# Cross-attention and a ternary feed-forward on one core: one f16 cast from VectorE to ScalarE, row maxima in PSUM, new instruction orders, feed-forward two steps earlier

## The reference

```
h = layernorm(x)
q = rmsnorm(h @ Wq) * gq ;  k = rmsnorm(ctx @ Wk) * gk ;  v = ctx @ Wv        # by head, D = 128
P = softmax(q @ k.T / sqrt(D))
x = x + (P @ v) @ Wo
y = quant8(layernorm(x)) ;  g = y @ tern(w_gate).T ;  u = y @ tern(w_up).T
h = rms_norm(silu(g) * u) * ln_weight
x = x + quant8(h) @ tern(w_down).T
```

## Time and profile before

| | |
|---|---|
| median of the runs | 529.06 us |
| profiled execution | 530.74 us, span 528.9 us |
| mean granted TensorE clock | 0.974 |
| PE busy | 420.7 us (80%) |
| weight loads busy | 316.9 us (60%) |
| DVE busy | 484.6 us (92%) |
| ACT busy | 428.1 us (81%) |
| POOL busy | 386.8 us (73%) |

### The profile page before, as it was taken

The page is one execution under the profiler, slowest core; times in us unless marked ns, Lnnn a source line. Parts: engine busy times, 40 slices in busy tenths (PEclk is TensorE's granted clock), DMA queues, the critical chain, the costliest instruction groups (busy, mean ns, idle before and its releaser), DMA issues.

```text
span 528.9 us, 14416 instructions
## 1 busy us (share of the span) xinstructions
PE 420.7 (80%) x4456; PEld 316.9 (60%) x4456; DVE 484.6 (92%) x1303; ACT 428.1 (81%) x1447; POOL 386.8 (73%) x312
## 2 busy tenths in 40 slices
PE   0248275699999999999999999999999556678885
PEld 0137264577777777677776777777777343345554
DVE  1989969899999999999999999999999857899995
ACT  1079488498988989889898898988989638799983
POOL 1015628479989899998989999899989943666772
PEclk9999877799999999999999999999999999899999
DMA  7950713154734445354444535445464530000001
GB/s 278 347 170 22 233 46 81 41 81 85 155 79 100 99 91 108 79 114 85 99 99 84 114 79 111 87 95 104 89 114 85 117 60 2 1 20 32 30 30 51
DMA packets 145324, 50.16 MB, mean 95 GB/s; under 512 B 135952, under 2 KB 143120, under 8 KB 144784
## 3 DMA queue, kind: packets, MB, share of 16 engines
q1 hardware_dynamic: 144192, 46.68, 39.7%
q10 hardware_dynamic: 1104, 3.15, 1.7%
HBM read 14.16 MB, written 2.10 MB: 31 GB/s over the span
## 4 chain that ended last, share of the span: by engine, by line
DVE 48%; issue 29%; POOL 11%; PE 5%; DMA 3%; ACT 3%; DVEq 1%; POOLq 0%; ACTq 0%
DVE khl L855 9%; DVE khl L837 5%; DVE qhl L812 3%; POOL work L476 3%; DVE smax L808 3%; POOL qshl L482 3%; POOL rkq L497 3%; DVE ham L914 2%; DVE nbias L820 2%; DVE ohl L830 2%; DVE work L979 2%; DMA xs<-in_x 2%; DVE phl L843 2%; DVE kqe L848 1%; PE KQ L1128 1%
## 5 line engine op out<-in xcount | busy, mean ns | idle before, releaser
L576 ACT ACTIVATE work<-SO,nbias,rkq 128x128 f32<-128x128 f32 x256 | 115.1, 479 | 23.9 <-DVE nbias L820 23.8
L351 PE MATMUL KQ<-hT,wqs 128*128 (+1 forms) x1536 | 104.3, 226 | 19.3 <-DVE qhl L812 7.2
L497 POOL TENSOR_TENSOR rkq<-kqe,negh 128x8 f32<-128x8 f32 x65 | 108.6, 1670 | 13.6 <-DVE kqe L848 13.6
L351 PEld LDWEIGHTS KQ<-hT,wqs 128*128 128x128 f16 x1536 | 95.0, 101 | 28.5 <-DVE qhl L812 11.0
L488 POOL TENSOR_TENSOR phl<-work,phl 128x512 f16<-128x512 f32 x64 | 74.1, 1158 | 45.3 <-DVE phl L843 45.3
L351 PE MATMUL EB<-As,ohl 128*128 128x256 f16 x768 | 94.3, 273 | 0.0
L351 PEld LDWEIGHTS EB<-As,ohl 128*128 128x128 f16 x768 | 75.0, 98 | 21.5 <-issue 0.2
L476 POOL TENSOR_TENSOR work<-work,rinv 128x512 f32<-128x512 f32 x64 | 70.0, 1094 | 7.2 <-DVE rinv L789 7.2
L482 POOL TENSOR_TENSOR qshl<-work,qshl 128x512 f16<-128x512 f32 x64 | 75.2, 1174 | 0.1
L351 PE MATMUL SO<-pT,cs 128*128 128x512 f16 x192 | 53.0, 386 | 11.5 <-DMA pT<-phl 10.5
L351 PE MATMUL SO<-kT,qhl 128*128 128x128 f16 x768 | 54.7, 222 | 9.0 <-ACT work L576 6.6
(11 more groups left out here) (159 smaller groups left out, 945.0 us busy)
## 6 DMA issues: line engine op xcount, KB each, us to landing
xs<-in_x SPq DMA_DIRECT2D x4, 512.0 KB, 10.6
wvo<-in_wo SPq DMA_DIRECT2D x1, 2048.0 KB, 18.9
out<-wqs SPq DMA_DIRECT2D x16, 128.0 KB, 1.7
raw<-in_ctxT ACTq DMA_DIRECT2D x1, 1024.0 KB, 5.5
stage<-in_wk SPq DMA_DIRECT2D x1, 1024.0 KB, 13.4
stage<-in_wq SPq DMA_DIRECT2D x1, 1024.0 KB, 16.3
stage<-in_wq ACTq DMA_DIRECT2D x1, 1024.0 KB, 12.7
kT<-khl SPq DMA_TRANSPOSE x64, 2.9
```

The lines of the kernel that those rows point to most:

```text
L351: last = matmul(out, lhsT=left(i), rhs=right(j), start=start and n == 0, stop=stop and n == 2)
L497: pool.tensor_tensor(rkq[:, g % 4, :], kqe[:, g % 2, :], negh[:, 0:2 * HG], ALU.pow).then_inc(root_ok, 1)
L576: ins = act.activation(pe[:, s, c], SB[:, c], ACT.Exp, scale=rkq[:, (g - AT_X + 1) % 4, HG + h:HG + h + 1], bias=nbias[:, s, h:h + 1], acc ...
```

## The change

P's high half is made by ACT (L625 of the changed kernel, the last instruction of its turn) and no longer by DVE. From turn 8 on `smax` lies in PSUM (`smax_ps`), and two constants lie there too (`c_psum`, set by DVE in turn 7), with which `pss` and `kqe` of k are formed; before, they were immediate numbers. All engines' blocks stand in another order inside a turn. The feed-forward begins with turn 66 instead of 68 and runs six of its turns beside the attention's last; for it GU writes `KQ` and `TM`, the hidden transposes `SO`, and the second part of the layer norm's statistics is two turns later.

```diff
-FFN_AT = NT + AT_O - AT_GU
+FFN_AT = NT + AT_X - AT_GU
...
-        smax = sb("smax", [P, 2, HG])
+        smax_sb = sb("smax", [P, 2, HG])
...
+        c_psum = TPf[:, 16:16 + 2 * HG].rearrange("p (s h) -> p s h", s=2)
+        smax_ps = TPf[:, 0:2 * HG].rearrange("p (s h) -> p s h", s=2)
+
+        def smax_of(b, s):
+            return smax_sb[:, s, :] if isinstance(b, int) and b < 2 else smax_ps[:, s, :]
...
-            for s in range(G):
-                step((FFN_AT + s) // G, (FFN_AT + s) % G)
-                ffn(0, s)
-            straight(ffn, G, 2 * G)
+            for s in range(2 * G):
+                if FFN_AT + s < NT + AT_E + 1:
+                    step((FFN_AT + s) // G, (FFN_AT + s) % G)
+                ffn(s // G, s % G)
...
+                if live(b, g, 0):
+                    s = g % 2
+                    need(pool, qsq_ok, b, g, 0)
+                    need(pool, ssq_ps, b, g, 0, 2)
+                    pool.tensor_tensor(qshl[:, s, 1, :], qsq[:, s, :], qshl[:, s, 0, :],
+                                       ALU.subtract).then_inc(qslo_ok, 1)
...
-                if live(b, g, 0):
-                    s = g % 2
-                    need(pool, qsq_ok, b, g, 0)
-                    need(pool, ssq_ps, b, g, 0, 2)
-                    pool.tensor_tensor(qshl[:, s, 1, :], qsq[:, s, :], qshl[:, s, 0, :],
-                                       ALU.subtract).then_inc(qslo_ok, 1)
...
-                if now(b, g) == G:
+                if now(b, g) == G + 2:
                     ffn_roots(1)
...
+                split(now(b, g))
...
+                if live(b, g, AT_X):
+                    s = (g - AT_X) % 2
+                    need(act, pn_ok, b, g, AT_X)
+                    need_dma(act, pT_in[s], b, g, AT_X, 2)
+                    act.copy(phl[:, s, 0, :], pn[:, s, :]).then_inc(phi_ok, 1)
...
+                    if now(b, g) == AT_GU:
+                        act.wait_ge(plo_ok, NT)
...
                     need(dve, pn_ok, b, g, AT_X, 2)
-                    dve.tensor_scalar(pss[:, s, :], psm[:, s, :], 1.0 / P_SCALE, None, ALU.mult).then_inc(pss_ok, 1)
+                    if isinstance(b, int) and b < 2:
+                        dve.tensor_scalar(pss[:, s, :], psm[:, s, :], 1.0 / P_SCALE, None,
+                                          ALU.mult).then_inc(pss_ok, 1)
+                    else:
+                        dve.tensor_tensor(pss[:, s, :], psm[:, s, :], c_psum[:, 0, :], ALU.mult).then_inc(pss_ok, 1)
...
-                if live(b, g, AT_X):
-                    s = (g - AT_X) % 2
-                    need(dve, pn_ok, b, g, AT_X)
-                    need_dma(dve, pT_in[s], b, g, AT_X, 2)
-                    dve.tensor_copy(phl[:, s, 0, :], pn[:, s, :]).then_inc(phi_ok, 1)
...
+                        dve.scalar_tensor_tensor(out=kqe[:, s, 0:HG], in0=kss[:, s, :], scalar=epsk[:, 0:1],
+                                                 in1=c_psum[:, 1, :], op0=ALU.add, op1=ALU.mult).then_inc(kse_ok, 1)
+                if now(b, g) == 7:
+                    dve.memset(c_psum[:, 0, :], 1.0 / P_SCALE).then_inc(cst_ok, 1)
+                    dve.memset(c_psum[:, 1, :], 2.0 ** -23).then_inc(cst_ok, 1)
+                    dve.wait_ge(cst_ok, 2)
...
-                    for s in (klo_ok, qlo_ok, exp_ok, olo_ok):
+                    for s in (klo_ok, qlo_ok, qse_ok, nb_ok):
...
-                    te.wait_ge(qse_ok, NT)
+                    for s in (exp_ok, olo_ok):
+                        te.wait_ge(s, NT)
...
-                    for banks, w in ((KQ, wgq), (SO, wuq)):
+                    for banks, w in ((KQ, wgq), (TM, wuq)):
...
-                        ins = te.transpose(TM[:, j * P:(j + 1) * P], hr[:, s, j * P:(j + 1) * P], ident_f[:, :])
+                        ins = te.transpose(SO[:, j * P:(j + 1) * P], hr[:, s, j * P:(j + 1) * P], ident_f[:, :])
```

More of the change, by code:

```diff
@@ L609, in step @@
                     ins.then_inc(ksq_ok, 1)
-                A_out(now(b, g))
                 if now(b, g) in range(B // XB):
                     c_high(g)
+                if live(b, g, AT_O):
+                    s = (g - AT_O) % 2
+                    need(act, o_ps, b, g, AT_O)
+                    need(act, e_ps, b, g, AT_O, 2)
+                    act.activation(ohl[:, s, 0, :], OB, ACT.Copy, scale=O_SHIFT).then_inc(ohi_ok, 1)
+                A_out(now(b, g))
                 if now(b, g) in range(3, 7):
@@ L1071, in step @@
                           lambda j: wks[:, j, g * GW:(g + 1) * GW], True, True).then_inc(k_ps, 1)
+                if live(b, g, AT_O):
+                    s, bb = (g - AT_O) % 2, batch(b, g, AT_O)
+                    if now(b, g) == AT_O:
+                        te.wait_ge(c_lo, 1)
+                        te.wait_ge(hlo_ok, 7)
+                    if now(b, g) == 2 * G - 1:
+                        te.wait_ge(c_lo, B // XB)
+                    need_dma(te, pT_in[s], b, g, AT_O)
+                    need(te, olo_ok, b, g, AT_O, 1)
+                    pairs(te.matmul, OB, lambda i: cs[:, i, bb, :], lambda j: pT[:, s, j, :],
+                          True, True).then_inc(o_ps, 1)
+                if now(b, g) == 1:
+                    te.wait_ge(wvo_in, 32)
+                    te.wait_ge(hlo_ok, 4)
+                ln_transposes(now(b, g) if now(b, g) >= 0 else None)
+                for i in range(*A_AT.get(now(b, g), (0, 0))):
+                    if i >= 4:
+                        te.wait_ge(A_cp, i - 3)
+                    wvo_product(i)
                 if live(b, g, AT_E):
@@ L1086, in step @@
                     ins.then_inc(e_ps, 1)
-                if now(b, g) == 1:
-                    te.wait_ge(wvo_in, 32)
-                    te.wait_ge(hlo_ok, 4)
-                for i in range(*A_AT.get(now(b, g), (0, 0))):
-                    if i >= 4:
-                        te.wait_ge(A_cp, i - 3)
-                    wvo_product(i)
+                if now(b, g) == 2 * G - 1:
+                    te.wait_ge(wsum_ok, 3)
+                    te.wait_ge(qse_ok, 2 * G - 1)
+                    te.matmul(MB[:, 8:11], lhsT=ones_f[:, :], rhs=absum[:, :], start=True, stop=True).then_inc(wgs_ok, 1)
                 if now(b, g) == 3:
```

195 lines of the change are left out of this document (88 added, 107 removed).

## The result

The changed kernel takes 539.15 us (median of four runs, 538.76 to 540.78) against 529.59 for the kernel before in the same comparison: 1.018 times as long, interval 1.014 to 1.022. It is slower, by 9.6; the forecast was 531.9, in a range of 519 to 541 (526 to 538 for the forecast's own case). The profiled execution took 538.87, its span is 537.1 us, 8.2 more than before.

What follows compares the result with a forecast made beforehand. The prediction saw five near-full queues and a ring of POOL and DVE's cast as the bound. Its terms, -8.0 + 13.1 + 1.0 + 0 - 3.3 = +2.8, gave 531.9 us for the median, range 519 to 541.

Steps and rivals of the forecast that it cites:

- the forecast's own case: Whole kernel: the summed terms, also with half the gain in turns 0 to 7 or rival D; 526 to 538, chance 0.64.
- the ring that was forecast: Turns 8 to 63: exponentials, q's squares on ACT, q's low half and P's normalisation on POOL, P's cast on ACT; 5.62 a turn.
- Term 1: Cast of P on ACT, turns 8 to 63: 5.62 a turn, 5.96 with a weight chunk; +13.1, plus +1.0 for loop branches.
- The +1.0 for loop branches: POOL's power at a loop's end lasts 1.82 against 1.63; twelve such are 2.3 if ACT pays the same, taken as +1.0.
- The sign given for this term: Changed timeline: ACT idles 0.3 to 0.4 before most P casts, released by POOL's normalisation, and not before exponentials.
- Rival A: Loop: ACT does not wait and falls to its bare sums, 303; kernel 515, or 521 with half the wait; chance 0.20.
- B: Loop: k's transposes, queued on SP behind P's, land late; 5.85 a turn, +13 more, kernel 545; chance 0.16.
- Term 2: Constants and maxima in PSUM, DVE's order: 0 in the loop, since POOL's and ACT's sums do not fall; bounds 0 and -2.
- rival D: The PSUM forms leave the lock; only nbias is longer, by up to 0.7, within its slack; sum unchanged; inside the 0.64.
- Term 3: Turns 0 to 7, where DVE sets the pace: its new order brings -8 at turn 8's exponentials; bounds -4 and -11.
- The subtracted wait of 1.0 in turn 7: Turn 7 on DVE: the weight mean waits for PE ahead of O's and k's low halves, costing about 1.0.
- Term 4: End of attention: first gate-and-up matmul 24.7 after turn 64's exponentials instead of 28.0; -3.3, bounds -6 and +1.

Runs made afterwards that it cites:

- Run 7: Changed kernel with only K's product ahead of the scores on PE: 539.38 us, ratio 1.018 to the kernel before.
- run 2: Changed kernel with P's normalisation ahead of q's low half on POOL, cast of P still on ACT: 537.15 us, ratio 1.011.
- Run 1: Changed kernel with only the cast of P back on DVE, behind kqe of k: 512.9 us, ratio 0.966.
- Run 11: Changed kernel with row maxima back in SBUF and the two constants as immediate numbers: 550.46 us, ratio 1.032.
- run 12: Changed kernel with the scale of A (turn 3) and the weight sums (turns 5 to 7) late again on DVE: 544.1 us, ratio 1.023.
- run 9: Changed kernel with cast of P on DVE, k's low halves ahead of it and O's low half, 16 filler matmuls in two PE gaps: 509.41 us, ratio 0.956.

## Why the prediction was right, and where its steps failed

Direction and range came true, and the ring that was forecast sets the pace. But the range of 519 to 541 holds faster, same and slower; 539.15 lies near its upper end and outside the 526 to 538 given for the forecast's own case; and it was 9.6 slower, not 2.8.

**Term 1 stands, a little small.** The loop cost 15.9 against 13.1 + 1.0. The turns without a chunk are 5.71, 5.70 and 5.62 against 5.62, the one with a chunk 5.96 to the hundredth. The 5.71 and the 5.70 have one hand-over each that is 0.08 longer: POOL starts 0.77 behind the second square's start instead of 0.69, or P's cast 1.15 behind the normalisation's instead of 1.08. The +1.0 for loop branches has nothing behind it: in the changed kernel every power of the middle lasts 1.64. The 1.82 was misread: in the kernel before it comes once in four turns, each time 0.10 behind the start of a DVE instruction of the weight chunk.

```profile
239.89 0.42 DVE L862 TENSOR_SCALAR raw<-stage  x1
```

The sign given for this term, ACT idle 0.3 to 0.4 ahead of most P casts, is not there as said: 0.25 to 0.33 stands ahead of the squares of k and 0.08 to 0.16 ahead of the cast. Run 7 shows where it went: a second ring of 5.56 lay under the first, through PE, and took most of the idle time to itself; with it open, the whole 0.43 is ahead of the cast. The text gave PE "0.6 of slack" by adding PE's own work, and did not ask what K waits for once O's cast no longer covers it. It changed nothing in the forecast, but run 2 shows that whoever had mended the first ring alone would have gained 3 and not the 15 to 19 expected. Rival A (ACT doesn't wait) fell; B (k's transposes late) too: PE's time lost to them is under 1 us in the changed loop. (A's "with half the wait 521" is a slip; half of the wait gives some 523.)

That +14.1 met +15.9 is not a measure of what the cast costs. Run 1 splits the 15.9: +25.7 for the cast on ACT and -9.8 for all the rest, which the prediction had at 0. The 5.62 came near because it adds up one turn of the changed kernel and does not start from the kernel before.

**Term 2 was right in the sum and wrong in its reason.** "I take 0", and rival D said that longer nbias lies "within its 1.4 of slack". The slack was counted to the exponentials only. Run 11: without the PSUM forms the new orders cost another 9.6. Put so: the cast's move costs, the PSUM forms save, and the 5.62 holds only with nbias at 0.15. The sum came out because term 1 had counted nbias at its short 0.15, not because the slack would have held.

**Term 3 was right in its sum**: -8.2 against -8, and run 12 finds 5.4 for the two places counted at 5.5. Its parts are off in both directions: the first exponentials, turn 4's, came 5.1 earlier (69.72 to 64.58) against 4.0, and turns 4 to 8 gained another 3.1 against 3.75. The subtracted wait of 1.0 in turn 7 didn't appear.

**Term 4 is the mis-sized term**: +0.3 instead of -3.3. Its clockwork holds up to there: the normalisation ends 4.0 after turn 64's exponentials (said: 3.85), exponentials 62 start at 10.8 (10.7), the scores of the last item at 13.6 (13.4). Then "scores, O, DVE's x1 to 16.7" came at 18.5, because O and E took 1.27 and 2.72, and "PE's O and E of turn 68 to 24.7" came at 28.25, because they took 1.38 and 2.62. I had put them at 0.81 and 1.47, their durations at the full clock, while the term's own times have PE idle for 4.08 and 4.24 in front of them (longest before, in that part: 2.94). Filled, the gaps give back 2.9 of the 3.6; the other 0.7 was not split.

The two profiled executions differ by 8.1 and the medians by 9.6, because the profiled execution before stood 1.1 above its median and the one after 0.3 below.

## What to carry to other kernels

Moving work off the full engine is worth nothing while it is put at the end of another engine's turn behind a result that comes late: look for the ring that closes through the new place, start to start, and then for the next ring 0.1 below it, since edits to parallel rings pay little until both are made (3.1 and 0.5 alone, 11.2 together). An engine that is 98% busy can still be waiting, in gaps too short for the profile to name. An engine off the bound can come back to it when its small instructions fall beside another's large ones. Where a plan opens idle time on TensorE, price the matmuls behind the gap at the lower clock, or fill the gap.

## What the runs showed of the hardware

- A cast of 512 f32 per partition on DVE took 0.41 to 0.42 when it started 0.79 or more into POOL's 1.64 power on 8 elements (run 9, 60 of 64), and 1.28 beside POOL's 1.15 subtraction of 512. The other way round, a power that started 0.08, 0.16 or 0.24 behind such a cast lasted 1.84, 1.75 or 1.67 instead of 1.64 (run 1, 34 times). So it matters which part of POOL's instruction DVE's falls on, and not only that one runs; why stays open.
- A DVE instruction of 4 elements, nbias, cost 0.15 beside POOL's power and 0.68 to 0.88 beside its 128x512 normalisation (before the change), and ended with the latter, 0.01 to 0.03 behind it. In run 11 nbias took 0.87 and `pss` 0.68 on average. With one operand in PSUM they took 0.15 and 0.16 in the changed kernel.
- The same 12 E matmuls took 1.47 at the full clock and 2.57 to 2.72 behind gaps of 4.08 to 4.24 us; two times 16 matmuls, 3.62 us each time, whose result nobody reads, made the kernel 4 us faster, of which 2.9 lie at these gaps.
